# A written-out second phase, a normalisation that runs one batch late, and re-placed expert steps in a three-layer decoder kernel

## The reference

```python
x = layernorm(x + attention(x))          # 16 heads, chunked linear attention, rope, gate
x = layernorm(x + expert(x, w1, w2))     # int8-quantised linear, silu(gate) * up, linear; weights of their own for each batch
x = layernorm(x + mixture(x))            # F = 1408 hidden, 8 low-rank adapters, the 2 best of them for each token
```

```python
s  = sqrt(max|x| / max|w|)                      # per channel
xs = x / s;  ws = w * s
xq = clip(round(xs / x_scale));  wq = clip(round(ws / w_scale))
out = xq @ wq.T * x_scale * w_scale.T
```

## Time and profile before

| | |
|---|---|
| median of 3 runs (lowest to highest) | 1132.95 us (1131.48 to 1133.48) |
| the profiled execution, own time | 1128.95 us |
| its span, first to last instruction | 1127.1 us |
| PE busy, share of the span | 1030.8 us, 91% |
| DVE, ACT, POOL busy | 64%, 36%, 26% |
| mean granted clock of TensorE | 0.977 |

### The profile page before, as it was taken

One profiled execution on the slowest core, in us unless ns is written; L12 is line 12 of the kernel. 1 busy time (PEld: TensorE's weight loads), 2 busy tenths in 40 slices (PEclk: granted clock), 3 DMA queues, 4 the chain that ended last, 5 costly groups with the idle time before them and its releaser, 6 DMA issues.

```text
span 1127.1 us, 13755 instructions
## 1 busy us (share of the span) xinstructions
PE 1030.8 (91%) x4920; PEld 809.6 (72%) x4920; DVE 717.8 (64%) x1150; ACT 402.7 (36%) x623; POOL 295.3 (26%) x245
## 2 busy tenths in 40 slices
PE   3799999989999827999999899999999999999997
PEld 2577777767777625777768687777777877888885
DVE  4565786785576646957657867764976774554542
ACT  3234333323342233344443253434253434322231
POOL 2247674543224400201222200142110132200021
PEclk9899999999999968999999999999999999999999
DMA  7116664130021025243463152446143327134421
...
DMA packets 47862, 142.98 MB, mean 127 GB/s; under 512 B 3497, under 2 KB 14633, under 8 KB 42161
## 3 DMA queue, kind: packets, MB, share of 16 engines
...
...
## 4 chain that ended last, share of the span: by engine, by line
PE 44%; DVE 13%; issue 3%; ACT 2%; POOL 1%; DMA 1%; DVEq 0%; ACTq 0%
PE f_h L106 7%; PE f_h L107 7%; PE f_h L108 7%; PE f_h L2172 4%; PE f_y L106 3%; PE f_y L107 3%; PE f_y L108 3%; DVE f_q_mem L1933 2%; DVE f_work L1913 1%; PE f_y L2362 1%; DVE f_work L1905 1%; PE f_z_sum L106 1%; PE f_z_sum L108 1%; PE f_z_sum L107 1%; PE f_z_second L107 1%
## 5 line engine op out<-in xcount | busy, mean ns | idle before, releaser
L106 PE MATMUL f_h<-f_xT_hi,f_up 128*128 128x512 f32 x352 | 140.5, 399 | 1.6 <-issue 0.9
L107 PE MATMUL f_h<-f_xT_hi,f_up 128*128 128x512 f32 x352 | 138.4, 393 | 0.0
L108 PE MATMUL f_h<-f_xT_lo,f_up 128*128 128x512 f32 x352 | 137.7, 391 | 0.0
L106 PE MATMUL ring<-w_hi,xT_hi 128*128 128x512 f32 x256 | 110.4, 431 | 24.4 <-POOL xT_lo L429 21.8
L1505 POOL TENSOR_TENSOR f_down_lo<-f_down_raw,f_down_hi 128x512 fp32r<-128x512 f32 x44 | 61.1, 1390 | 227.5 <-ACT f_down_hi L1555 227.5
L1710 ACT ACTIVATE f_work<-f_h 128x512 f32<-128x512 f32 x88 | 52.4, 596 | 171.4 <-PE f_h L2172 114.8
L1905 DVE TENSOR_TENSOR f_work<-f_work,f_weightT 128x512 f32<-128x512 f32 x88 | 65.1, 739 | 73.7 <-ACT f_work L1710 69.9
L1516 POOL TENSOR_TENSOR weights<-weights,f_rows 128x512 f32<-128x512 f32 (+1 forms) x24 | 31.9, 1360 | 299.9 <-ACT f_rows L1637 183.6
L1913 DVE TENSOR_TENSOR f_work<-f_h,f_work 128x512 f32<-128x512 f32 x88 | 60.8, 691 | 70.8 <-PE f_h L108 65.3
L107 PE MATMUL ring<-w_hi,xT_lo 128*128 128x512 f32 x256 | 103.7, 405 | 0.0
L108 PE MATMUL ring<-w_lo,xT_hi 128*128 128x512 f32 x256 | 103.5, 404 | 0.0
...
## 6 DMA issues: line engine op xcount, KB each, us to landing
...
f_x<-x_scratch SPq DMA_DIRECT2D x7, 1024.0 KB, 8.8
...
x_tok<-in_x SPq DMA_DIRECT2D x4, 1024.0 KB, 5.6
...
```

The lines of the kernel that those rows point to most:

```text
L106: pe.matmul(out, lhs_hi, rhs_hi, start=start, stop=False)
L107: pe.matmul(out, lhs_lo, rhs_hi, start=False, stop=False)
L108: return pe.matmul(out, lhs_hi, rhs_lo, start=False, stop=stop)
```

## The change

- **First phase, ACT:** the rounding of the first tokens, `x_hi(0)`, goes ahead of the first eight weight chunks. `channel_rows` goes from behind `v_out(g+1)` to behind `exponential(g+1)` in tiles 7 and 12. `qT_out` goes ahead of `deviation` at a batch's end.
- **First phase, POOL:** the four pieces of `scale_weights` run together behind the rotations; two ran ahead of them.
- **First phase, DVE:** `channel_top(0, 1)` of tile 6 is two halves, one behind `mask_state(6, 1)` and one behind `attT_lo(6)`. The row scales, roundings and clamps of `which` 0 stand half a tile to one tile later, those of (1, 1) half a tile earlier.
- **Second phase:** all four batches are written out; statistics of the expert layer stand behind `activation(b, 10, 0)` and their variance at the start of `between`; variance, square root and normalisation of batch b run in tile 0 of batch b+1, with the store behind it; the last batch is normalised in two halves.

```diff
@@ -467,3 +467,3 @@
-            def scale_weights(which, pieces):
+            def scale_weights(which):
                 C = CHANNELS[which]
@@ -473,3 +473,3 @@
                     pool.wait_ge(up_stored[1], PRIMED + 32 * SPLIT[1])
-                for t in pieces:
+                for t in range(TT):
                     pool.tensor_tensor(scaled[1][:, t, 0:C], w_raw[:, t, 0:C], rows[:, 1, 0:C], ALU.mult)\
@@ -493,6 +493,2 @@
                 jobs = {where: j for j, where in JOBS.get(g, [])}
-                if g == 8:
-                    scale_weights(0, (0, 1))
-                if g == 13:
-                    scale_weights(1, (0, 1))
                 if has_next(g):
@@ -503,5 +499,5 @@
                 if g == 8:
-                    scale_weights(0, (2, 3))
+                    scale_weights(0)
                 if g == 13:
-                    scale_weights(1, (2, 3))
+                    scale_weights(1)
                 residual(g)
@@ -648,5 +644,5 @@
+            x_hi(0)
             weight_hi(0)
             weight_hi(1)
-            x_hi(0)
             x_hi(1)
@@ -691,8 +687,4 @@
                     v_out(g + 1)
-                if g == 7:
-                    channel_rows(0)
                 if g == 9:
                     transposed_out(0, 0)
-                if g == 12:
-                    channel_rows(1)
                 attT_hi(g)
@@ -700,2 +692,6 @@
                     exponential(g + 1)
+                if g == 7:
+                    channel_rows(0)
+                if g == 12:
+                    channel_rows(1)
                 if g == 13:
@@ -715,6 +711,6 @@
                     expert_normalise()
-                if ends_batch(g):
-                    deviation(batch_of(g))
                 if more:
                     qT_out(g + 1)
+                if ends_batch(g):
+                    deviation(batch_of(g))
                 if has_next(g, 2):
@@ -855,4 +851,5 @@
-            def channel_top(which, i):
-                C = CHANNELS[which]
+            def channel_top(which, i, part=0, parts=1):
+                C = CHANNELS[which] // parts
+                channels = slice(part * C, (part + 1) * C)
                 if i == 0 and which == 0:
@@ -863,3 +860,4 @@
                     dve.wait_ge(ew_loaded[which], PRIMED + 16)
-                dve.tensor_reduce(top[:, i, 0:C], expert_tokens(i, which)[:, :, 0:C].rearrange("p t c -> p c t"),
+                dve.tensor_reduce(top[:, i, channels],
+                                  expert_tokens(i, which)[:, :, channels].rearrange("p t c -> p c t"),
                                   AX.X, ALU.max, apply_absolute_value=True).then_inc((x_top_ready, w_top_ready)[i][which], 1)
@@ -964,6 +962,8 @@
                     channel_ratio(0)
-                if g == 8:
-                    row_scale(0, 0)
                 if g == 9:
-                    row_scale(0, 1)
+                    round_rows(0, 0)
+                    clamp(0, 0)
+                if g == 10:
+                    round_rows(0, 1)
+                    clamp(0, 1)
                 if g == 11:
@@ -976,2 +976,4 @@
                     row_scale(1, 1)
+                    round_rows(1, 1)
+                    clamp(1, 1)
                 if g == 15:
@@ -979,2 +981,4 @@
                 mask_state(g, 1)
+                if g == 6:
+                    channel_top(0, 1, 0, 2)
                 if g == 7:
@@ -982,5 +986,5 @@
                 if g == 8:
-                    round_rows(0, 0)
+                    row_scale(0, 0)
                 if g == 9:
-                    round_rows(0, 1)
+                    row_scale(0, 1)
                 if g == 11:
@@ -992,5 +996,2 @@
                     clamp(1, 0)
-                if g == 14:
-                    round_rows(1, 1)
-                    clamp(1, 1)
                 attend(g)
@@ -1004,7 +1005,3 @@
                 if g == 6:
-                    channel_top(0, 1)
-                if g == 8:
-                    clamp(0, 0)
-                if g == 9:
-                    clamp(0, 1)
+                    channel_top(0, 1, 1, 2)
                 if g == 11:
@@ -1418,9 +1416,5 @@
             prepare(0)
-            with eng.Fori(0, B - 2) as b:
-                hidden(b, True)
-                between(b, True, True)
-            hidden(B - 2, True)
-            between(B - 2, True, False)
-            hidden(B - 1, False)
-            between(B - 1, False, False)
+            for b in range(B):
+                hidden(b, b < B - 1)
+                between(b, b < B - 1, b < B - 2)
@@ -1429,2 +1423,6 @@
+        def norm_part(b, half):
+
+            return (b, slice(0, TT)) if half is None else (b + half, slice(2 * half, 2 * half + 2))
+
         prime(nc, primed, used)
@@ -1475,2 +1473,4 @@
                     load_up(f + SLOTS)
+                    if f == 0 and b:
+                        store(b - 1)
                     if f == 0:
@@ -1596,5 +1597,6 @@
-            def deviation(b):
-                sc.wait_ge(var_ready, PRIMED + b + 1)
-                sc.activation(rstd[:, 1, :], rstd[:, 0, :], ACT.Sqrt).then_inc(std_ready, 1)
+            def deviation(b, half=None):
+                n, tokens = norm_part(b, half)
+                sc.wait_ge(var_ready, PRIMED + n + 1)
+                sc.activation(rstd[:, 1, tokens], rstd[:, 0, tokens], ACT.Sqrt).then_inc(std_ready, 1)
@@ -1722,2 +1724,6 @@
                     silu_out(b, f, 0)
+                    if f == 0 and b:
+                        if expert:
+                            root(b, 0)
+                        deviation(b - 1)
                     if expert and f == 2:
@@ -1786,5 +1792,5 @@
                 next_down(b, 10)
-                if another:
-                    root(b + 1, 0)
-                deviation(b)
+                if not expert:
+                    deviation(b, 0)
+                    deviation(b, 1)
@@ -2054,6 +2060,10 @@
                         clamp_x(b, 1)
-                    if expert and f == 10:
-                        expert_statistics(b)
+                    if f == 0 and b:
+                        variance(b - 1)
                     weighted(b, f, 0)
                     activation(b, f, 0)
+                    if f == 0 and b:
+                        if expert:
+                            channel_scale(b, 0)
+                        normalise(b - 1)
                     if expert and f == 1:
@@ -2075,3 +2085,3 @@
                     if expert and f == 10:
-                        expert_variance(b)
+                        expert_statistics(b)
                     weighted(b, f, 1)
@@ -2096,21 +2106,22 @@
-            def normalise(b, expert, another):
-                dve.wait_ge(x3_loaded, PRIMED + 32 * b + (32 if expert else 16))
-                for t in range(TT):
-                    dve.wait_ge(y_ready, PRIMED + b * TT + t + 1)
-                    dve.tensor_tensor(x3[:, t, :], y_ps[t][:, :], x3[:, t, :], ALU.add).then_inc(y_added, 1)
-                    dve.wait_ge(y_added, PRIMED + b * TT + t + 1)
-                    last = dve.bn_stats(stats[:, t, :], x3[:, t, :])
-                if another:
-                    channel_ratio(b + 1, 0)
-                link = waiter(norm_step, b * 4)
-                link(last)
-                moments(dve, stats, part, mean[:, :], rstd[:, 0, :], link).then_inc(var_ready, 1)
-                dve.wait_ge(std_ready, PRIMED + b + 1)
-                link(dve.reciprocal(rstd[:, 2, :], rstd[:, 1, :]))
-                for t in range(TT):
+            def add_tokens(b, t):
+                dve.wait_ge(y_ready, PRIMED + b * TT + t + 1)
+                dve.tensor_tensor(x3[:, t, :], y_ps[t][:, :], x3[:, t, :], ALU.add).then_inc(y_added, 1)
+                dve.wait_ge(y_added, PRIMED + b * TT + t + 1)
+                dve.bn_stats(stats[:, t, :], x3[:, t, :]).then_inc(stats_ready, 1)
+
+            def variance(b, half=None):
+                n, tokens = norm_part(b, half)
+                dve.wait_ge(stats_ready, PRIMED + b * TT + tokens.stop)
+                moments(dve, stats[:, tokens, :], part[:, tokens, :], mean[:, tokens], rstd[:, 0, tokens],
+                        waiter(norm_step, n * 3)).then_inc(var_ready, 1)
+
+            def normalise(b, half=None):
+                n, tokens = norm_part(b, half)
+                link = waiter(norm_step, n * 3 + 2)
+                dve.wait_ge(std_ready, PRIMED + n + 1)
+                link(dve.reciprocal(rstd[:, 2, tokens], rstd[:, 1, tokens]))
+                for t in range(tokens.start, tokens.stop):
                     dve.tensor_scalar(x3[:, t, :], x3[:, t, :], mean[:, t:t + 1], rstd[:, 2, t:t + 1],
                                       ALU.subtract, ALU.mult).then_inc(normed, 1)
-                if another:
-                    channel_scale(b + 1, 0)
@@ -2118,2 +2129,3 @@
                 if expert:
+                    expert_variance(b)
                     expert_shift(b)
@@ -2131,3 +2143,15 @@
```

(14 more changed lines are left out.)

20 lines of the change are left out of this document (11 added, 9 removed).

## The result

The changed kernel takes 1147.66 us in the median of 4 runs (1142.61 to 1150.13), against 1132.72 (1131.48 to 1133.48). The ratio is 1.0134, interval 1.0112 to 1.0156: 15 us slower, where 1.7 on that scale was forecast, within a range that ended at 1141.

A forecast was written before the change was run, and what follows sets the result against it. PE bounds the kernel, busy 1030.8 of 1127.1 us, so only its waits and lower clock matter. The terms summed to +1.5 on 1128.95, giving 1130.4, or 1134.4 on the median's scale; range 1126.5 to 1141.

The forecast's parts named there:

- Tile 10: Second phase, three batches: statistics no longer ahead of the activation, 1.2 us a batch kept, -2.8 in all, ends 0 and -7.1.
- Tiles 13 to 15: End of the first phase: down-weight steps of tiles 13 and 14 lie under PE's work, so 0.
- the collision of POOL and DVE: Rival: POOL's one-piece weight scaling in tiles 8 and 13 slows DVE's rotations, 3.0 us to lose, 1137.4; chance 0.10, slower.
- The start: Rounding the first tokens first lets PE start at about 12.6 instead of 18.54 us: -5.7, ends -5.3 and -5.9.
- The turns: Second phase between batches: 0 to 1 gains 6.0, less 1.0 given back, -5.0; 1 to 2 +1.0; 2 to 3 0.
- the next item: Turn of batch 1 to 2: normalisation behind the first activation delays DVE's later work, +1.0 us, ends 0 and +1.9.
- a wait at tile 0 to 2: Second phase, start of a batch: a new wait there replacing the loop's would prove the prediction wrong; no size given.
- Tile 6: First phase: the halved reduction waits for the weights' transfer ahead of `attend(6)`; PE stalls 5.0, net +3.4, plus 2.5 clock.
- Tiles 7 and 12: First phase: gate products wait for the row copy behind both exponentials, +3.7 us each, plus 2.5 of clock each.
- Tile 8: First phase: roundings no longer ahead of `attend(8)`, so PE's wait for `att` goes: -2.1 and -1.7 of clock.
- The end: Behind the last product: two normalised tiles remain in place of four, -0.5 us, ends 0 and -1.0.
- The clock: Rival: no clock fall follows the three new first-phase stalls, so 7.5 us goes, 1126.9; chance 0.17, faster.

The follow-up runs named there:

- b_stats: Kernel before, with only the expert layer's statistics moved behind tile 10's first activation and their variance to the start of `between`: 1136.83 against 1131.94 us, ratio 1.0045.
- a_normfirst: Changed kernel, with ACT running `expert_normalise` and its store ahead of `next_down(3)`: 1137.27 us against 1133.17 for the kernel before, ratio 1.0035.
- a_split: Changed kernel, with POOL's `scale_weights` in two pieces again, around the rotations of tiles 8 and 13: 1138.40 us against 1133.17 for the kernel before, ratio 1.0060.
- b_start: Kernel before, with only the rounding of the first tokens moved ahead of the first eight weight chunks: 1126.92 against 1131.94 us, ratio 0.9953.
- b_defer: First phase of the kernel before with the changed second phase, but expert statistics left where they were: 1131.18 us against 1133.17 for the kernel before, ratio 0.9977.
- after2: The changed kernel unaltered, timed again: 1144.77 us against 1132.34 for the kernel before, ratio 1.0116.
- best2: Before with first tokens earlier, batches written out, expert statistics moved, `expert_normalise` ahead of `next_down(3)`, and `which` 0 row scales, roundings, clamps later: 1115.24 us, ratio 0.9852.

## Why the prediction was wrong, step by step

**Tile 10: the step that failed.** The prediction had the mechanism in its hand: `expert_normalise` stands behind `next_down(3)`, and that behind its transfer. It then wrote "The transfer is issued only a little earlier when PE is", and kept a gain of 1.2 a batch. The transfer is issued behind ACT's part of the second activation, and the four statistics, moved from ahead of the first activation to ahead of the second, leave that one where it was: ACT's issue is 13.0 later than before (584.14, where PE's difference ahead of the tile was 12.7). So nothing at all is gained at `x_transposed`; PE merely waits there for what it no longer waits for in the tile. The end of that term at 0 ("the transfer holds all") should have been its middle, and even that end left out the clock: one wait of 2.41 became two, of 1.21 and 3.54, and the second was followed by a low clock in batch 0 (0.59 over 6.4 us, 2.6 lost) and in batch 1 (0.72 over 6 us, 1.7 lost). `b_stats` and `a_normfirst` show both halves: 4.9 us lost alone, and 9 to 11 us back from the changed kernel with ACT's order mended, with no wait left at `x_transposed`. The sign was wrong: +6.1 in the first execution and +4.1 in the second, for -2.8. That the wait in the tile shrinks by just the 1.2 a batch that the prediction kept is luck: its own list had these waits "gone", and it is POOL beside DVE that leaves 1.2 of them standing.

**Tiles 13 to 15: taken at nothing.** I had the collision of POOL and DVE as a rival, priced it by tile 8, and asked for it ahead of `att`. In tile 8 it did come there (`att` took 1.60 for 0.69, at 237.28), but PE didn't wait for it. It cost PE 0.80 at the next features, and 1.04 in tile 13, ahead of `q_mem`, where a rotation took 0.97 longer (`a_split`). The rival was right in kind and wrong in place and size. The rest of the stage's 3.9 is for the most part clock: its window at 367.4 stood at 0.74 (6.6 us, 1.7 lost), and that fall also comes in versions that don't touch the stage. So only 1.0 of the 3.9 is shown to be the change's.

**The start.** The bound was the right one, DVE's first low part. But I read DVE's time from a trace in which POOL was idle beside it. POOL's work moved there with ACT's, and cost 0.95: the first matmul comes 4.8 earlier in the changed kernel and 5.0 in `b_start`, for 5.9. The -4.0 at the end of tile 5 has 0.8 of clock on top (30 to 45 us stands at 0.66, in `b_start` at 0.77). By `b_start`'s median, 5.0, the 5.7 is not refuted; its reason is.

**The turns.** The branch is gone as forecast, and the difference falls by 5.9 there, the forecast's 6.0. Then it rises again by 3.1 at tile 1. The prediction gave back 1.0 for "the next item", and named "a wait at tile 0 to 2" among what would make it wrong; `b_defer` has this wait too: 1.8 of it is the late normalisation's, and 1.2 goes with `f_scale`, beside POOL. DVE's chain of tile 1 had no slack for 1.92, which the idle time of the earlier trace rows couldn't show: that idle time lies ahead of the place, not behind it.

**Tile 6** was forecast as +3.4 and 2.5 of clock, 4.2 came: the stall was 4.30 for 5.0, since the weights landed 6.7 after issue for 7.1, and the clock cost 1.7 (0.72 over 6 us), a size error. **Tiles 7 and 12** were right: waits of 4.40 and 4.21, which is 3.7 more than before in both, and low clocks behind both. Those falls were deep in this execution (0.58 and 0.51) and less so in `after2` (0.72 behind both). **Tile 8** paid back less than the forecast's 3.8: 4.4 is gained up to 241 us, of which 1.7 is lost again at once, for the most part in waits of 0.80 for the features and 0.44 for the next product, and `best2` gains 2.4 by the same move. **The end** was right within 0.3: 0.6 is gained behind the last product, and 0.4 lost ahead of it.

**The clock** as a rival that "holds" is out: PE's busy time grew by 10.5. It was the right kind of term, 2.5 a stall, but counted for three stalls of the first phase alone, and the change made stalls of about 3 us in five more places (`q_mem`, tile 1 of batch 1, and three times `x_transposed`).
